# Gated delta attention on one Trainium2 core: one projection moved from the start of a slot to its middle a slot earlier, key scaling moved late in ScalarE's order

## The reference, cut to what matters

```python
q, k, v = split(silu(causal_conv4(x @ W_qkv)))      # 4 taps along the sequence
z       = x @ W_z
q, k    = l2norm(q) * DK ** -0.5, l2norm(k)
for t in range(T):                                   # state S is 128 x 128 for each value head
    S = S * exp(g[t])
    u = (v[t] - k[t] @ S) * beta[t]
    S = S + outer(k[t], u)
    o[t] = q[t] @ S
out = (rmsnorm(o) gated by silu(z)) @ W_out          # layer 0 gates after the norm, layer 1 before
```

## Time and profile before

| | us |
|---|---|
| median of 3 runs (4843.72 to 4848.77) | 4845.57 |
| the profiled execution's own time | 4845.66 |
| its span, first to last instruction | 4843.9 |
| L1233 (once in a slot), first and last start, layer 0 | 733.4 to 2388.7 |
| the same, layer 1 | 3091.6 to 4792.4 |

### The profile page before, as it was taken

One profiled execution on the slowest core, in us unless ns is written; L12 is line 12 of the kernel. 1 busy time (PEld: TensorE's weight loads), 2 busy tenths in 40 slices (PEclk: granted clock), 3 DMA queues, 4 the chain that ended last, 5 costly groups with the idle time before them and its releaser, 6 DMA issues. The chain is left out here.

```text
span 4843.9 us, 93590 instructions
## 1 busy us (share of the span) xinstructions
PE 4399.0 (91%) x32596; PEld 3630.6 (75%) x32596; DVE 3855.8 (80%) x8126; ACT 2985.7 (62%) x9834; POOL 985.5 (20%) x1252
## 2 busy tenths in 40 slices
PE   4999939999999999999969997499999999999998
PEld 3578827888888888888835876488888888888787
DVE  6938988888888888888741689788888888888886
ACT  1146626777777777777611664466676767676665
POOL 0024411221212112121200433021211121121211
PEclk7999969999999999999979999799999999999999
DMA  1035642222222222222210565222222222222222
GB/s 56 30 91 173 188 138 70 82 79 79 88 74 81 73 82 85 78 83 73 60 31 20 160 190 170 84 83 74 72 82 72 82 75 82 78 81 73 78 74 65
DMA packets 580414, 422.57 MB, mean 87 GB/s; under 512 B 392808, under 2 KB 476312, under 8 KB 579502
## 3 DMA queue, kind: packets, MB, share of 16 engines
q1 hardware_dynamic: 563566, 408.20, 28.8%
q0 software_dynamic: 16384, 8.42, 1.0%
HBM read 296.24 MB, written 120.16 MB: 86 GB/s over the span
## 5 line engine op out<-in xcount | busy, mean ns | idle before, releaser
L1225 DVE SCALAR_TENSOR_TENSOR conv_l<-mix_l,taps_l,conv_l 128x512 f32<-128x512 f32 x1152 | 854.6, 751 | 238.7 <-ACT conv_l L1047 207.6
L854 PE MATMUL pj_l<-x_high,w_high_l 128*128 128x512 f32 x1280 | 584.8, 457 | 159.5 <-ACT w_high_l L1056 159.5
L1428 POOL TENSOR_TENSOR fac_l<-den_l,powers 128x4 f32<-128x4 f32 x256 | 257.2, 1006 | 1818.5 <-DVE den_l L1349 1816.9
L854 PE MATMUL pj_l<-x_low,w_high_l 128*128 128x512 f32 x1280 | 511.9, 400 | 0.0
L1193 ACT ACTIVATE Z_l<-gb_l 128x128 f32<-128x128 f32 x1024 | 267.3, 284 | 395.2 <-PE gb_l L1012 394.3
L854 PE MATMUL pj_l<-x_high,w_low_l 128*128 128x512 f32 x1280 | 510.6, 399 | 0.0
L637 POOL DMA_DIRECT2D own_dram<-key_kkS_l x512 | 294.8, 582 | 923.8 <-ACT key_kkS_l L509 913.5
L1021 PE MATMUL gb_l<-wo_l,gT_l 128*128 128x256 f32 x2048 | 474.2, 383 | 0.0
L1021 PEld LDWEIGHTS gb_l<-wo_l,gT_l 128*128 128x128 f32 x2048 | 375.1, 190 | 62.3 <-ACT Z_l L1193 12.8
L1359 DVE SCALAR_TENSOR_TENSOR x<-gb_l,fac_l,x 128x256 f32<-128x256 f32 x1024 | 413.0, 476 | 9.4 <-POOL fac_l L1428 3.6
L854 PEld LDWEIGHTS pj_l<-x_high,w_high_l 128*128 128x128 f32 x1280 | 241.8, 189 | 221.1 <-ACT w_high_l L1056 159.9
(11 more groups left out here) (204 smaller groups left out, 10702.2 us busy)
## 6 DMA issues: line engine op xcount, KB each, us to landing
rows_l<-rows_dram SPq DMA_DIRECT2D x128, 1024.0 KB, 5.6
k_dram<-kT_l SPq DMA_DIRECT2D x128, 256.0 KB, 2.4
kk_dram<-key_kkS_l SPq DMA_DIRECT2D x128, 256.0 KB, 2.4
kq_l<-k_dram SPq DMA_DIRECT2D x128, 256.0 KB, 3.3
kkS_l<-kk_dram SPq DMA_DIRECT2D x128, 256.0 KB, 5.8
w_raw_l<-in_wx SPq DMA_DIRECT2D x32, 640.0 KB
lane_k_l<-own_dram SPq DMA_DIRECT2D x32, 512.0 KB, 4.1
t_dram<-lane_t_l SPq DMA_DIRECT2D x14, 1024.0 KB, 4.9
```

What stands on the lines that cost most here:

```text
L854: ins = nc.tensor.matmul(pj_bank(c, t), wt[:, k, t, :], xt[:, k, :, at], start=(k == 0 and n == 0), stop=(k == KD - 1 and n == 2))
L1225: ins = nc.vector.scalar_tensor_tensor(out, mix[:, t, :, i:i + P], wt(i), out, ALU.mult, ALU.add)
L1428: nc.gpsimd.tensor_tensor(fac[:, g, :], den[:, g, :], m.powers[:, 1, :], ALU.pow).then_inc(fac_ok[g], 1)
```

## The change: what it does

On PE the first projection (t = 0, six matmuls) is no longer made at the start of the slot for the next chunk; it is made after L997 and ahead of `values_token_major`, for the next chunk but one. So every chunk's projection 0 is made in the slot before the one that made it. A pair of calls ahead of the first slot makes that of chunk 1. On POOL the halo moves likewise: from the start of the slot to behind `norm_columns`, for the next chunk but one. On ACT both groups' scaled keys move from the start of the slot to behind the SiLU of the values, ahead of the second weight splits and of y; `ktok` gets two buffers, and the wait of `square_keys` is one chunk looser. `silu_z` of group 0 moves behind `copy_corner` for c > 0. DVE's and SP's lists are unchanged.

```diff
--- before.py
+++ after.py
@@ -674,7 +674,7 @@
         sq_kq = diag_b[:, :, :].rearrange("p g n -> p (g n)")
         decay = sb("decay", [P, GROUPS, WIDE])
         ap = sb("ap", [P, 2, GROUPS, BATCH, 2, P])
-        ktok = sb("ktok", [P, WIDE])
+        ktok = sb("ktok", [P, 2, WIDE])
         ke = sb("ke", [P, GROUPS, WIDE])
         vn = sb("vn", [P, GROUPS, WIDE])
         qd = sb("qd", [P, GROUPS, BATCH, P])
@@ -903,7 +903,6 @@
                             project(nh, ncn, t, 0, False)
                             project(nh, ncn, t, 1, False)
 
-                    fill(0)
                     if not first:
                         pe.wait_ge(res_ok[0], BATCH * it - BATCH // 2)
                     pe.wait_ge(ap_ok, 6 * it + 2)
@@ -997,6 +996,9 @@
                             ins = nc.tensor.matmul(gb[:, 1, g, bank(b)], y[:, g, bank(b)], ap[:, c % 2, g, b, 1, :],
                                                    start=(c == 0), stop=True, skip_group_check=True)
                         ins.then_inc(o_mm[g], 1)
+                    if it < KHEADS * CHUNKS - 2:
+                        project(*following(nh, ncn), 0, 0, False)
+                        project(*following(nh, ncn), 0, 1, False)
                     if not last:
                         values_token_major(nh, ncn)
                     for g in range(GROUPS):
@@ -1029,6 +1031,8 @@
                 keys_token_major(0, 0, True)
                 queries_token_major(0, 0, True)
                 key_products(0, 0)
+                project(0, 1, 0, 0, False)
+                project(0, 1, 0, 1, False)
                 values_token_major(0, 0)
                 steps(body)
 
@@ -1080,8 +1084,8 @@
                     q = 4 * h + c
                     act.wait_ge(ktok_mm, q + 1)
                     if not first:
-                        act.wait_ge(ke_ok, 6 * h + 2 * c)
-                    nc.scalar.activation(ktok[:, :], kk[:, 0, :], ACT.Copy).then_inc(ktok_cp, 1)
+                        act.wait_ge(ke_ok, 6 * h + 2 * max(0, c - 1))
+                    nc.scalar.activation(ktok[:, q % 2, :], kk[:, 0, :], ACT.Copy).then_inc(ktok_cp, 1)
                     square(0).then_inc(k_sq, 1)
 
                 def square_queries(h, c):
@@ -1106,7 +1110,7 @@
                     act.wait_ge(decay_ok, 2 * q + g + 1)
                     for b in range(BATCH):
                         last = decay[:, g, (b + 1) * P - 1:(b + 1) * P]
-                        ins = nc.scalar.activation(ke[:, g, bank(b)], ktok[:, bank(b)], ACT.Copy, scale=last)
+                        ins = nc.scalar.activation(ke[:, g, bank(b)], ktok[:, q % 2, bank(b)], ACT.Copy, scale=last)
                     ins.then_inc(ke_ok, 1)
 
                 def copy_z32(it):
@@ -1144,13 +1148,9 @@
                 def body(h, c, first, last):
                     it = 4 * h + c
                     nh, ncn = following(h, c)
-                    if c < CHUNKS - 1:
-                        scaled_keys(h, c, 0)
                     if not last:
                         copy_mix(nh, ncn, 0, False)
                     copy_z32(it)
-                    if c < CHUNKS - 1:
-                        scaled_keys(h, c, 1)
                     if not last:
                         copy_mix(nh, ncn, 1, False)
                         square_keys(nh, ncn, False)
@@ -1164,11 +1164,10 @@
                     if c == 2 and h < KHEADS - 1:
                         for t in range(CONVS):
                             split_weights(h + 1, t)
-                    if not last:
-                        silu_z(nh, ncn, 0)
                     if c > 0:
                         copy_corner(it)
                     if not last:
+                        silu_z(nh, ncn, 0)
                         square_queries(nh, ncn)
                     if c == 0:
                         copy_corner(it)
@@ -1176,6 +1175,9 @@
                         silu_z(nh, ncn, 1)
                         for t in range(1, CONVS):
                             silu_conv(nh, ncn, t)
+                    if c < CHUNKS - 1:
+                        for g in range(GROUPS):
+                            scaled_keys(h, c, g)
                     if c == 2 and h < KHEADS - 1:
                         for t in range(CONVS, PROJS):
                             split_weights(h + 1, t)
@@ -1403,8 +1405,6 @@
                 def body(h, c, first, last):
                     it = 4 * h + c
                     nh, ncn = following(h, c)
-                    if not last:
-                        halo(nh, ncn, False)
                     if c > 0:
                         pool.wait_ge(rows_in[c % 2], 16 * (2 * h + c // 2 + 1))
                         pool.wait_ge(kk_mm, it + 1)
@@ -1421,6 +1421,8 @@
                         nc.gpsimd.tensor_tensor(flat(wo), flat(wo_raw), norm, ALU.mult).then_inc(wo_ok, 1)
                     if not last:
                         norm_columns(nh, ncn)
+                    if it < KHEADS * CHUNKS - 2:
+                        halo(*following(nh, ncn), False)
                     for g in range(GROUPS):
                         pool.wait_ge(den_ok[g], it + 1)
                         if not first:
@@ -1431,6 +1433,7 @@
                 pool.wait_ge(taps_in, 48)
                 halo(0, 0, True)
                 norm_columns(0, 0)
+                halo(0, 1, False)
                 steps(body)
```

## The result

The changed kernel takes 4867.92 us (median of 5 runs, 4865.71 to 4869.74), the kernel before on the same chip 4847.93 (5 runs, 4843.72 to 4850.47). The ratio is 1.0045, with a 95% interval of 1.0033 to 1.0057: slower by 20 us, where 4835 was forecast and 4864 was the upper end. The profiled execution has a span of 4866.5 us.

A forecast was written before the change was run, and what follows sets the result against it. No engine is full (PE 91%, DVE 80%, ACT 62%); two almost equal chains, DVE's and PE's, bound each slot. First layer +11.8, second -20.0, first slots -2.2: total -10.4 us from 4845.66, so 4835, 8-in-10 range 4808 to 4864.

The forecast's parts named there:

- The gap at the start of a slot: Slot start: DVE's first convolution no longer waits for ACT's copy, gaining 1.11 to 1.68 us at each start.
- The projection in its new place: PE, ahead of the turned values: 1.4 us, moving that chain by 1.4 minus what PE idled there before.
- the keys in chunk 0: ACT, chunk 0: scaled keys ahead of y delay y by 2.2 us; DVE's decay scan waits 1.8 us.
- the splits in chunk 2: Chunk 2: keys delay ACT's second weight splits, DVE waits 0.5 us for their high parts, tail moves by 0.52.
- `silu_z`: ACT, chunk 3: done behind `copy_corner`, ahead of `square_queries`, it costs DVE 0.38 us more.
- the rival of the slow key block: ACT, chunks 0 and 2: keys taking 2.67 us or more put the total over 4855; chance 0.2.
- PE's clock falls: Chunk 0, after PE idles 2.2 us: 1.2 GHz for projection and output matmuls, about +150 us, 4985; chance 0.03.

The follow-up runs named there:

- e1: Changed kernel plus six PE matmuls with unused results in chunk 0, ahead of the wait for ACT's copy of y: 4840.87 us, 0.9984 of the kernel before.
- e3: Changed kernel with the scaled keys of chunk 0 alone back in their old places: 4799.84 us, 0.9903 of the kernel before.
- e2: Changed kernel with chunk 0's moved projection placed in PE's idle time, ahead of L992: 4803.31 us, 0.9906 of the kernel before.
- e7: Changed kernel with projection and halo back at the slot's start, only ACT's part kept: 4966.9 us, 1.0248 of the kernel before.
- e5: e2 with `silu_z` of group 0 ahead of `copy_corner` again: 4797.3 us, 0.9901 of the kernel before.
- e6: e2 with chunk 2's second weight splits ahead of the scaled keys: 4784.22 us, 0.9876 of the kernel before.

## Why the prediction was wrong

**The gap at the start of a slot: right.** It closed everywhere. In the changed kernel the first two taps of a slot's first convolution wait for ACT in the first slots of a layer alone. In chunks 1 to 3 this pair of taps now takes 1.62 to 1.86 instead of 1.54, with POOL's `qd` still running as it starts; in chunk 0, which has no `qd`, it takes 1.53. That was not foreseen, and no run takes `qd` away.

**The projection in its new place, the keys in chunk 0, the splits in chunk 2, `silu_z`: right in place and size.** The changed kernel's rows for chunks 2 and 3:

```profile
1244.58 0.76 DVE L1368 TENSOR_TENSOR w_low_l<-w_raw_l,w_high_l 128x256 fp32r<-128x256 f32 x2 [0.57 <-ACT w_high_l L1060]
...
1250.39 0.89 PEld L894 LDWEIGHTS kk_l<-eye,vT_l 128*128 128x128 f32 x8 [0.18 <-DVE ap_l L1282]
...
1257.94 1.63 DVE L1227 SCALAR_TENSOR_TENSOR conv_l<-mix_l,taps_l,conv_l 128x512 f32<-128x512 f32 x2
...
1267.77 0.17 DVE L1247 TENSOR_SCALAR qcol_l<-ss_kq_l 128x4 f32<-128x4 f32 x1 [0.89 <-ACT diag_b_l L1079]
...
1276.39 0.86 PEld L894 LDWEIGHTS kk_l<-eye,vT_l 128*128 128x128 f32 x8 [0.43 <-DVE ap_l L1282]
```

The second L1368 waits 0.57 (0.52 predicted), and L894 is held by DVE and not by the projection. In chunk 3 L1247 waits 0.89 (0.84 predicted) where it waited 0.46, and L894's idle time is down from 1.16 to 0.43, still ended by DVE. In chunk 0 the keys took 2.33 from their start to y's, against 2.34 in the sum, so the rival of the slow key block falls. That is 0.29 us an ACTIVATE, and the trace does not agree with the 0.41 that the prediction worked out, as an estimate, from the Trainium skill's page "ScalarE: Activation LUTs", section "Rules for kernel authors". Leaving the clock out, both layers come out as added up: layer 0 lengthened by 19.8 us between its first and last L1235, of which 5 x 1.63 is the clock, leaving 11.6 (predicted 10.7); layer 1 by 3.6, less 14 x 1.63, leaving -19.2 (predicted -21.1).

**The step that failed** is the rival "PE's clock falls", which I gave 0.03: "the longest idle quoted from a slot is 1.16, at full clock", and from that I concluded that 2.2 would do nothing. The sum had put the idle time in the right place with nearly the right length (2.2 against 2.38) and then had no term for it. Nothing in the trace of before had such an idle time inside a slot, so it could not say what it costs; that should have been a cost bounded from both sides and not a rival at 3 in 100. The rival's own price was off as well, too high in both of its factors. I had the clock low for the projection and the outputs, 4.7 us in all 32 slots. It was low for 3.41 us of L992 and L996 and cost 1.63, in 19 slots: 31 us and not 150. Added to the 4835, that gives 4866, against 4868 measured.

The Trainium skill's page "TensorE: Matmul & The Clock Gate", section "HAM oscillation — how this bites in real kernels", tells of a loop in which PE's wait, there for a DMA, brings the clock down for the next burst of matmuls. Here the trace agrees for a wait for ACT, with 2.31 to 2.38 us of idle and a lower clock in 19 of 32 slots, and e1 shows that filling half of it is enough.

## What to carry to other kernels

When a move makes PE wait for another engine in the middle of a dense stretch, price the low clock of the work behind the wait as well as the wait; here it cost 1.63 us on top of 2.4, and decided the sign. Where a loop has slots of different kinds, go through an in-order list for each kind: the keys' late place was free in chunk 1, where ACT still idles 0.7 before y, held DVE up by 0.57 us in chunk 2 and y by 2.3 in chunk 0, and an order that depends on the chunk (e3) turned 0.45% lost into 1% won. And if such an idle time can't be avoided, put work in it that must be done anyway (e2), which serves twice.

## What the runs showed of the hardware that was not expected

- The same idle time, 2.31 to 2.38 us ahead of y's matmuls, brought the granted clock down in 5 of 16 chunk-0 slots of layer 0 and in 14 of 16 of layer 1, and in e7, after 2.29 to 2.32 us, in 4 and 13. The slots are the same instruction for instruction within a layer, and a slot has either 3.65 or 5.28 us for its block, nothing between. No run was made to settle what picks them.
- With 1.20 to 1.22 us of idle (e1) the clock fell in none of 32 slots, and with the 1.15 to 1.23 of e2, e5 and e6 in none of 96.
- The clock fell when work had come back, not in the idle time itself: the window of the wait shows 1.00, the first microsecond behind it 0.72. In the 19 slots it fell 0.13 to 1.42 us after the first load of L992, in the 17 of e7 0.00 to 1.32 us after that of its L993.
